# Convolution blocks 128 bytes apart and in another order, in a four-layer residual kernel on one core

## What is computed

```
x = x + conv(x, W0, 9 taps, 4 groups of 32 channels) + c @ cw0.T + side
x = x + (sum_k att0[b, k] * E0[k]) @ x + att0 @ bias_k0      # att0 = softmax(MLP(c)), K = 8
x = x + (sum_k att1[b, k] * E1[k]) @ x + att1 @ bias_k1
x = x + conv(x, W3, 9 taps, 4 groups of 32 channels) + c @ cw3.T + side
```

## Time and profile before

| | |
|---|---|
| median of 3 runs | 2548.66 us (2548.07 to 2548.96) |
| the profiled execution, its own time | 2548.97 us |
| its span in the trace | 2547.1 us |
| mean granted clock of TensorE | 0.996 of full |
| TensorE, ACT, DVE busy | 99%, 88%, 78% |
| DMA queue 1 | 87.3% of 16 engines |

### The profile page before, as it was taken

How to read it: one execution, slowest core, us unless ns; L and a number is a source line. 1 busy time by engine, 2 the same in 40 slices (tenths; PEclk the granted TensorE clock), 3 DMA queues, 4 the chain that set the end, 5 groups by cost and what they waited for, 6 DMA issues and landing times.

```text
span 2547.1 us, 43755 instructions
## 1 busy us (share of the span) xinstructions
PE 2520.7 (99%) x11068; PEld 2062.1 (81%) x11068; DVE 1995.5 (78%) x5032; ACT 2252.2 (88%) x2449; POOL 16.0 (1%) x27
## 2 busy tenths in 40 slices
PE   7999999999999999999999999999999999999997
PEld 6888888888888888888888888888888888888886
DVE  8777787778777878787877778777877787888784
ACT  6889998999899989998998899899989998998895
POOL 2000000000000000000000000000000000000000
PEclk9999999999999999999999999999999999999999
DMA  7889889888888888899889888988888888888986
GB/s 257 318 332 331 328 324 334 329 328 325 332 328 327 329 333 326 325 333 328 329 326 333 330 329 324 333 329 329 325 333 329 327 327 333 325 326 333 329 312 235
DMA packets 334986, 825.56 MB, mean 324 GB/s; under 512 B 37370, under 2 KB 39426, under 8 KB 302210
## 3 DMA queue, kind: packets, MB, share of 16 engines
q1 hardware_dynamic: 332736, 823.94, 87.3%
q10 hardware_dynamic: 2242, 1.53, 0.2%
HBM read 137.97 MB, written 134.23 MB: 107 GB/s over the span
## 4 chain that ended last, share of the span: by engine, by line
PE 97%; DVE 1%; DMA 1%; ACT 1%; SPq 0%; issue 0%; ACTq 0%; DVEq 0%
PE pair L930 82%; PE quad L980 14%; PE pair L970 1%; DVE partial L754 0%; DMA x_ch<-x_ph 0%; DMA mix<-att_saved 0%; ACT x_ch L473 0%; ACT x_out L525 0%; DVE operands L790 0%; DMA x_ph<-in_small 0%; DVE operands L787 0%; DMA x_ph<-x_ch 0%; SPq L318 0%; SPq L370 0%; DVE operands L714 0%
## 5 line engine op out<-in xcount | busy, mean ns | idle before, releaser
L930 PE MATMUL pair<-operands 128*128 128x512 f32 x9216 | 2157.3, 393 | 3.4 <-DVE operands L805 1.8
L930 PEld LDWEIGHTS pair<-operands 128*128 128x128 f32 x9216 | 1722.6, 188 | 385.8 <-DVE operands L805 2.2
L473 ACT COPY x_ch<-x_in 128x1088 f32<-128x1088 f32 x255 | 556.9, 2184 | 0.0
L787 DVE CAST operands<-x_ch 128x512 fp32r<-128x512 f32 x512 | 205.4, 422 | 437.4 <-DMA x_ch<-x_ph 437.4
L525 ACT COPY x_out<-x_ch 128x1024 f32<-128x1024 f32 x252 | 524.2, 2080 | 0.2 <-DMA x_ch<-x_ph 0.2
L542 ACT ACTIVATE x_ph<-pair,bias_now 128x512 f32<-128x512 f32 x508 | 354.8, 699 | 187.6 <-PE pair L930 187.6
L533 ACT ACTIVATE x_ph<-pair,bias_now 128x512 f32<-128x512 f32 x512 | 357.5, 698 | 77.5 <-PE pair L930 69.7
L754 DVE SCALAR_TENSOR_TENSOR partial<-expert,mix,partial 128x128 f32<-128x128 f32 x1536 | 416.4, 349 | 0.0
L980 PE MATMUL quad<-operands 128*128 128x512 f32 x1536 | 372.9, 392 | 2.4 <-DVE operands L790 2.4
L805 DVE TENSOR_TENSOR operands<-x_ph,operands 128x542 fp32r<-128x542 f32 x512 | 357.7, 721 | 0.0
L980 PEld LDWEIGHTS quad<-operands 128*128 128x128 f32 x1536 | 289.7, 189 | 66.6 <-issue 3.1
(11 more groups left out here) (77 smaller groups left out, 214.2 us busy)
## 6 DMA issues: line engine op xcount, KB each, us to landing
x_ch<-x_ph SPq DMA_DIRECT2D x1024, 256.0 KB, 3.0
x_ph<-x_ch SPq DMA_DIRECT2D x512, 272.0 KB, 2.9
x_ph<-x_ch SPq DMA_DIRECT2D x512, 271.0 KB, 2.6
x_in<-in_x SPq DMA_DIRECT2D x128, 1024.0 KB, 5.7
out<-x_out SPq DMA_DIRECT2D x128, 1024.0 KB, 4.3
x_out<-in_W SPq DMA_DIRECT2D x8, 144.0 KB, 4.4
expert<-in_e ACTq DMA_DIRECT2D x2, 512.0 KB, 8.5
mix<-att_saved SPq DMA_DIRECT2D x2, 512.0 KB, 6.8
```

The source lines that it names most:

```text
L473: nc.scalar.copy(to, of).then_inc(x_cut, 1)
L930: mm = nc.tensor.matmul(conv_bank[g % 2], w[l][:, m, g, :], x[:, g, m * SEG:m * SEG + N], start=(m == 0 and x is hi and w is w_hi), stop=( ...
```

## The change

`SEG` goes from 16 to 32. A row has 32 halo columns a side (`ROW` = 576, runs of 16 columns), and the three blocks start 128 bytes apart. The weight matrices are laid out by block, then group, with 32 columns between blocks, so that block `m` starts `m` x 128 bytes (and whole multiples of 512) into its tile; x's groups now start 2304 bytes apart. The blocks of a convolution are taken in the order 0, 2, 1 in groups 0 and 2 and 1, 0, 2 in groups 1 and 3. To make room, `ones` and `att_t`, which are used at the start alone, move into spare columns of `x3_ch`.

```diff
-    SEG = 16
+    SEG = 32
...
-        NEXT_BLOCK = C + SEG
-        NEXT_GROUP = BLK * C + ROW - N
-        WEIGHTS = G * BLK * C + C
+        NEXT_BLOCK = G * C + SEG
+        NEXT_GROUP = C
+        WEIGHTS = BLK * NEXT_BLOCK - SEG
...
-        ones = sb("ones", [C, C])
...
-        att_t = [sb(f"att_t{l}", [K, B]) for l in range(2)]
...
+        att_t = [spare[0:K, (4 + l) * B:(5 + l) * B] for l in range(2)]
+        ones = spare[:, 6 * B:7 * B]
...
             def conv(l, g, hi, lo, done):
-                for m in range(BLK):
+                order = (0, 2, 1) if g % 2 == 0 else (1, 0, 2)
+                for m in order:
                     for w, x in ((w_hi, hi), (w_hi, lo), (w_lo, hi)):
                         mm = nc.tensor.matmul(conv_bank[g % 2], w[l][:, m, g, :], x[:, g, m * SEG:m * SEG + N],
-                                              start=(m == 0 and x is hi and w is w_hi),
-                                              stop=(m == BLK - 1 and w is w_lo))
+                                              start=(m == order[0] and x is hi and w is w_hi),
+                                              stop=(m == order[-1] and w is w_lo))
                 mm.then_inc(done, 1)
```

## The result

The changed kernel takes 2612.8 us (median of 4 runs, 2611.83 to 2615.2) against 2548.73 us for the kernel before: a ratio of 1.0254, interval 1.0237 to 1.027, or 64 us. The forecast was 2574. The sign is as forecast, and the time lies inside the stated range of 2530 to 2640. It lies outside the 2560 to 2590 that the prediction gave for its own case, and the change costs 2.5 times what was predicted. The profiled execution took 2612.26 us, its span is 2610.4, the granted clock 0.997 (0.996 before), so the clock has no part in it.

A forecast was written before the change was run, and what follows sets the result against it. TensorE bounds at 19.53 us a step, but ACT's loop (19.53 - 0.23 + 0.451 - 0.02) becomes 19.73: 0.20 longer, 25 us over 125 steps, plus 0.5, on 2548.97 gives 2574 us. Range 2530 to 2640.

The forecast's parts named there:

- two anchors: ACT waits on TensorE at conv4's and conv1's group 0; 0.21 us of room at conv1, loop 0.23 shorter than the step.
- TensorE's gain: Convolution matmuls get faster with the new block starts and order: 0.14 us a step, alone 18 us.
- The gain is lost as TensorE waits for ACT at conv4's start: TensorE waits for ACT's evacuation of x1 (L533) at conv4's start, some 0.2 us a step.
- The cast, the edges: On ACT, the longer cast of x adds 0.107 us a step, the four edge evacuations of x3 0.109.
- DMA: The twelve moves after x3's evacuation carry longer rows and take 0.3 us more, between 0 and 0.42.
- The strided copies: On ACT, the two cuts add 0.235 us a step at an unchanged price per element; joins stay at 2080 ns.
- rival B: Strided copies pay partly per inner run, 0.18 us a copy, joins near 2260 ns: 2665 us; chance 0.18.
- The second loop: x3 evacuation, twelve DMA moves, split_x1 and low_x on DVE, then conv1: 19.66 us a step, so it adds nothing.
- Rival A: Wider steps free ACT's strided copies of contention, TensorE sets the pace: faster, 2537 or down to 2515 us; chance 0.24.
- C (no change): A late weight load hides 0.1 us and room is 0.1 larger: within 5 us of 2549; chance 0.08.
- D (TensorE slower): Odd groups' x and weights conflict, slowing TensorE's reads by over 0.07 us a step; counted with the forecast.

The follow-up runs named there:

- experiment 3: Kernel of before with only the join's reads moved to 128 bytes apart instead of 64, still in 32 runs of 32: 2569.27 us.
- Experiment 9: Changed kernel with low_x made in four operations, one a group, TensorE waiting for its own group alone: 2612.0 us, 1.0242.
- experiment 16: Changed kernel, low_x by groups, joins along segments, x3 halo columns on GpSimd, two x moves ahead of x3, two behind x1's first: 2538.45 us, 0.9954.
- experiments 12 and 13: 12: changed kernel, low_x by groups, copies along segments, x3 halo columns on GpSimd: 2607.06 us. 13: likewise, cuts unaltered, x moves before x3 moves: 2620.32 us.
- experiment 7: Changed kernel with the blocks in the order 0, 1, 2 in all groups: 2614.13 us, 1.0257.

## Why the prediction was right or wrong

- **What bounds the kernel now: right.** TensorE sets the pace, ACT has two anchors and little room. Padding ACT measured 0.27 us of room for the predicted 0.23. But the prediction took the two rooms as one sum: work behind the first anchor can't use the 0.21 there, so the joins' growth alone costs 20 us (experiment 3). In the changed kernel both anchors are overrun, and the sum holds.
- **TensorE's gain: right in size, in part wrong in its reason.** 0.14 a step, 18 us, were predicted; with ACT out of the way the two parts together bring 14 us (2552.51 to 2538.45), 0.11 a step. The reason given was that the order halves the changes between odd and even multiples of 128 bytes. At 64 bytes the same order halves the like changes and loses 9 us, so counting them isn't enough.
- **The gain is lost as TensorE waits for ACT at conv4's start: right,** with the line, L533, and the place.
- **The cast, the edges: right,** 0.11 and 0.11 against 0.107 and 0.109.
- **DMA: right,** 0.31 against 0.3.
- **The strided copies: the mis-sized term, and the step that failed.** The prediction said "if a stride of 128 bytes costs what 64 does", took that, and left the joins at 2080. 0.235 were predicted, 0.60 measured: 0.27 more for the two joins, 0.10 more for the two cuts. Alone the assumption nearly holds (2004 and 2033). Beside matmuls and DVE together it does not (2089 and 2186), and the join's step alone, in the real loop, gives the joins' whole growth (experiment 3). For the cuts no run separates the step from the 64 elements more; that their 0.10 has the same cause is argued. The three rows that were to show the price independent of the step went from 16 to 64 bytes, all from the trace of before. They could not show what lies beyond, and the term had a range on paper only in rival B.
- **The sum with that term put right:** 19.53 - 0.27 + 0.82 - 0.02 = 20.06 us a step; measured are 20.02, and 125 x 0.50 = 62 of the 64 us. The rest of the argument stands.
- **The second loop: too short in the prediction.** It was put at 19.66 and showed itself at 19.91 once the copies were shorter. Part of the difference is the copies' price, which this loop shares; how the rest is divided was not tried. One sign of being wrong that the prediction named did appear: in the step shown of the changed kernel it is low_x's end that releases the start of conv1. Experiment 9 took that wait away, and the time stayed. A third loop, from the x3 moves through the x moves to the cast, wasn't listed at all. Neither set the time of the change itself, as ACT's loop was longer than both; they decide what any relief of ACT brings.
- **Rival A (faster, contention freed) fell,** on the other side: the change adds contention. It had rightly asked whether copies are slowed by their neighbours: 2099 ns in a quiet stretch against 2186 was that effect, seen at 64 bytes. The rule of the Trainium skill ("SBUF — State Buffer", two separate sides) that ACT and TensorE never wait for each other at the SBUF would have made a join the same in all stretches; the runs show 2033 ns alone and 2136 beside matmuls. That is a measured slowing; no run shows at which part of the chip it arises.
- **Rival B (2665, much slower) was nearer in size, and its mechanism fell.** It priced inner runs, "joins near 2260"; joins came at 2242. But 64 runs of 16 cost what 32 of 32 do (2078 for 2080), and the step, with the runs as they were, costs 101 ns. A row that fits a rival's number isn't yet its mechanism. It was for B that the range went up to 2640, so that the measured time lies inside it is luck.
- **C (no change) fell:** the room was larger by 0.04, not by 0.1, and the addition was thrice the room.
- **D (TensorE slower) fell:** its groups take 2050 ns, less than the 2070 of before.

What stays open: why a strided copy on ACT depends on its step so much more beside other engines than alone, why one order of the blocks gains at 128 bytes and loses at 64, and why the cuts, which write with the long step, take more from matmuls (200 ns) than the joins, which read with it. Which of the edits behind experiment 16 are needed wasn't tried one by one.

## What to carry to other kernels

A price per element read from rows of one layout doesn't carry to another stride where other engines work beside it: measure the copy beside them (and look in the trace that they do run, and that no other does), or give the term a range that holds a dearer one. Where an engine off the bound has 0.2 us of room in 19.5, every longer row there is a cost of the change, however well the bounding engine does; and where it meets the bound twice in a step, each stretch has its own room. Relief on one engine pays in full only once every loop of waits is shorter than the bound: here that took three edits and the right place of two transfers in a queue, and two of the steps on the way (experiments 12 and 13) were slower than the one before them.

## What the runs showed of the hardware

- ACT's contiguous copy of 1024 elements (fp32) takes 1044 ns, one with elements at 64 or 128 bytes 2004 to 2035, whatever its runs. Beside matmuls: 1052, 2010 to 2041 (64 bytes) and 2132 to 2136 (128 bytes). Beside DVE alone the 128-byte join takes 2072 and 2088. Beside both the 64-byte join takes 2089, the 128-byte one 2184 and 2187. DMA changes nothing (2004 and 2034).
- Alone, DVE is faster at such copies: the cut of 1088 elements takes it 1133 ns where ACT takes 2078, the cut of 1152 elements with 128-byte steps 1293 where ACT takes 2176.
- TensorE's groups of nine matmuls of 512 columns (the three of experiment 7) take 2050 ns (128 bytes between blocks, the order of the change), 2060 to 2070 (128 bytes, natural), 2070 (64 bytes, natural) and 2066 to 2106 (64 bytes, the order of the change). The order of addresses alone moves a kernel that TensorE bounds by 11 us in 2549.
